# Attention queries for two tiles at once in a two-layer kernel, x transposed in pairs

## The reference, cut to what matters

```python
x = x + attention0(layernorm(x), ctx)          # q = xn @ Wq.T + bq, k, v from ctx, 16 heads of 16
x = x + ffn_sine(layernorm(x))                 # 256 -> 1024 -> 256
x = x + attention1(ctx, layernorm(x), mask)    # the same with a mask of 1024 x 77 for each batch
x = x + ffn_fp4(layernorm(x))                  # gate, up and down, 704 wide, values rounded to 4-bit floats
# attention: scores = q @ k.T / 4 per head, softmax over 77 keys, times v, then @ Wo + bo
```

## Time and profile before

| | before |
|---|---|
| median of 3 runs | 1034.82 us |
| runs | 1032.75 to 1035.31 us |
| profiled execution | 1034.89 us, span 1033.1 us |
| mean granted TensorE clock | 0.978 of full |
| TensorE matmuls busy | 961.5 us, 93% |
| VectorE busy | 834.7 us, 81% |
| ACT busy | 497.0 us, 48% |
| GpSimd busy | 467.5 us, 45% |

### The profile page before, as it was taken

How to read it: one execution, slowest core, us unless ns; L and a number is a source line. 1 busy time by engine, 2 the same in 40 slices (tenths; PEclk the granted TensorE clock), 3 DMA queues, 4 the chain that set the end, 5 groups by cost and what they waited for, 6 DMA issues and landing times. The chain is left out here.

```text
span 1033.1 us, 18658 instructions
## 1 busy us (share of the span) xinstructions
PE 961.5 (93%) x6532; PEld 869.5 (84%) x6532; DVE 834.7 (81%) x2049; ACT 497.0 (48%) x1061; POOL 467.5 (45%) x663
## 2 busy tenths in 40 slices
PE   6899999999589999998899999999957999999997
PEld 5899999999478888887699999999846888888885
DVE  4989999997499999986677777777666898898874
ACT  2554443433288888886344433333244544444442
POOL 1235445451366666653221211211026777777762
PEclk9999999999799999999999999999979999999999
DMA  9020000000000000001000000000000000000000
GB/s 348 10 93 2 2 2 1 1 2 2 0 1 1 2 1 1 1 1 44 7 1 2 1 2 1 2 1 1 2 1 0 21 2 22 21 22 21 22 21 21
DMA packets 6076, 18.21 MB, mean 18 GB/s; under 512 B 864, under 2 KB 2784, under 8 KB 5472
## 3 DMA queue, kind: packets, MB, share of 16 engines
q1 hardware_dynamic: 5264, 16.52, 4.2%
q10 hardware_dynamic: 720, 0.50, 0.2%
HBM read 12.83 MB, written 4.19 MB: 16 GB/s over the span
## 5 line engine op out<-in xcount | busy, mean ns | idle before, releaser
L662 ACT COPY a_xTs<-a_psQ 128x256 f32<-128x256 f32 x64 | 23.9, 373 | 266.4 <-PE a_psQ L734 266.4
L726 PE MATMUL a_psS<-kblk,a_qTs 128*128 128x308 f32 (+2 forms) x768 | 148.0, 338 | 1.4 <-DVE a_qTs L561 1.4
L795 PEld LDWEIGHTS a_psO<-vblk,a_prob 128*128 128x128 f32 x1280 | 148.4, 192 | 0.0
L795 PE MATMUL a_psO<-vblk,a_prob 128*128 128x51 f32 (+1 forms) x1280 | 148.2, 271 | 0.0
L1387 PE MATMUL f_psGU<-wgu,f_xTs 128*128 128x512 f32 (+1 forms) x576 | 141.3, 391 | 3.9 <-ACT f_silu L1339 2.7
L499 DVE TENSOR_REDUCE a_mx<-a_psS 128x6 f32<-128x462 f32 (+1 forms) x192 | 111.8, 583 | 19.6 <-PE a_psS L726 12.4
L726 PEld LDWEIGHTS a_psS<-kblk,a_qTs 128*128 128x128 f32 x768 | 119.2, 193 | 5.3 <-DVE a_qTs L561 1.6
L1387 PEld LDWEIGHTS f_psGU<-wgu,f_xTs 128*128 128x128 f32 x576 | 103.7, 192 | 19.9 <-DVE f_xTs L1151 4.6
L635 POOL TENSOR_TENSOR a_rstd<-a_mv,expo 128x1 f32<-128x1 f32 x64 | 16.4, 256 | 228.8 <-DVE a_mv L573 228.8
L1013 PEld LDWEIGHTS s_psY<-w,s_hid 128*128 128x128 f32 x768 | 97.4, 188 | 18.0 <-POOL s_hid L931 14.2
L1013 PE MATMUL s_psY<-w,s_hid 128*128 128x256 f32 x768 | 102.3, 282 | 6.7 <-POOL s_hid L931 6.7
(11 more groups left out here) (152 smaller groups left out, 1916.4 us busy)
## 6 DMA issues: line engine op xcount, KB each, us to landing
out_x<-x SPq DMA_DIRECT2D x8, 512.0 KB, 2.6
x<-in_x SPq DMA_DIRECT2D x3, 1024.0 KB, 12.5
w<-in_w SPq DMA_DIRECT2D x1, 2304.0 KB, 9.0
w<-in_w SPq DMA_DIRECT2D x2, 1024.0 KB, 17.3
a_mask<-in_mask SPq DMA_DIRECT2D x4, 308.0 KB, 4.0
wat<-in_att SPq DMA_DIRECT2D x1, 1024.0 KB, 20.3
x<-in_x SPq DMA_DIRECT2D x1, 768.0 KB, 8.5
wat<-in_att SPq DMA_DIRECT2D x2, 256.0 KB, 5.1
```

The costliest lines, as they stand in the source:

```text
L726: mm = nc.tensor.matmul(psS[n][:, (a - h0) * KV:(b - h0) * KV], qTs[:, u, p, k, :], kblk[:, r, t // R, k, (a - 8 * k) * KV:(b - 8 * k) * K ...
L795: mm = nc.tensor.matmul(psO[:, CH[c] * VW:(CH[c] + n) * VW], prob[:, v, c * P:(c + 1) * P], vblk[:, t // R, c * NJ * VW:(c * NJ + n) * VW] ...
```

## The change

Queries are made for a pair of tiles. In an even step i TensorE makes four x transposes, those of tiles i + 2 and i + 3, which fill the whole bank psQ; ACT copies all 512 columns to xTs, which is single now; and `queries(i + 2)` makes the first 128 query rows of both tiles at once, 256 columns wide, in the left half of psQ. In the odd step that follows there are no x transposes and no x copy, and `queries` makes the other 128 query rows, in the right half, after VectorE has read the left. ACT's bias (L683) and VectorE's low part (L561) are one instruction of 256 columns a step. qTs holds two pairs. Scores of a tile take their 128 of the 256 columns and wait for both halves.

All that comes before is moved: bn_stats, bn_aggr and the GpSimd pair to tile i + 5, normalise and the bias row to tile i + 4, and the steps begin at -5. VectorE runs steps -5 and -4 ahead of the key lows, step -3 ahead of the first keys, and steps -2 and -1 after the bias row (and the first mask). The waits for x loads are moved with bn_stats. vT is a view of the prob buffer, which is not written by exp before step 1.

The diff, cut (the headings after @@ say where):

```diff
@@ class Context: vT is handed in instead of allocated
-        self.vT = ctx.enter_context(nc.sbuf_tensor(f"b{l}_vT", [P, KC, B, 3 * KV], F32))
+        self.vT = vT
@@ attention, tiles
-        xTs = sb("xTs", [P, 2, KC * P])
-        qTs = sb("qTs", [P, 2, 2, KC, P], F32R)
+        xTs = sb("xTs", [P, KC, 2 * P])
+        qTs = sb("qTs", [P, 2, 2, KC, 2 * P], F32R)
...
-        FIRST, LAST, LOOP_FROM, LOOP_TO = ATT_FIRST, ATT_LAST, ATT_LOOP_FROM, ATT_LOOP_TO
+        FIRST, LAST, LOOP_FROM, LOOP_TO = ATT_FIRST - 2, ATT_LAST, ATT_LOOP_FROM, ATT_LOOP_TO
...
-        context = Context(nc, sem, g, l, ctx, psS[0:2], psT, (psO, psY))
+        vT = prob[:].rearrange("p u n -> p (u n)")[:, 0:KC * B * 3 * KV].rearrange("p (h b n) -> p h b n", h=KC, b=B)
+        context = Context(nc, sem, g, l, ctx, psS[0:2], psT, (psO, psY), vT)
@@ VectorE
-                def normalise(t, u):
+                def normalise(t):
+                    u = t % 2
                     wait(dve, rstd_ready, t + 1)
-                    wait(dve, xT_mm, t - 1)
+                    wait(dve, xT_mm, t // 2)
...
-                    if valid(i + 3):
-                        nc.vector.bn_stats(st[:, v, :], x[:, i + 3, :]).then_inc(st_set, 1)
-                        wait(dve, st_set, i + 4)
+                    if valid(i + 5):
+                        nc.vector.bn_stats(st[:, v, :], x[:, i + 5, :]).then_inc(st_set, 1)
+                        wait(dve, st_set, i + 6)
...
-                    if valid(i + 1):
-
-                        wait(dve, q_high, i + 2)
-                        for k in range(KC):
-                            last = nc.vector.scalar_tensor_tensor(
-                                qTs[:, v, 1, k, :], psQ[:, k * P:(k + 1) * P],
-                                cols[:, C_BQ + 2 * l + k:C_BQ + 2 * l + k + 1], qTs[:, v, 0, k, :].bitcast(F32),
-                                ALU.add, ALU.subtract)
-                        last.then_inc(q_low, 1)
+                    if valid(i + 2):
+                        s, h = (i + 2) // 2, i % 2
+                        wait(dve, q_high, i + 3)
+                        nc.vector.scalar_tensor_tensor(
+                            qTs[:, s % 2, 1, h, :], psQ[:, h * 2 * P:(h + 1) * 2 * P],
+                            cols[:, C_BQ + 2 * l + h:C_BQ + 2 * l + h + 1], qTs[:, s % 2, 0, h, :].bitcast(F32),
+                            ALU.add, ALU.subtract).then_inc(q_low, 1)
...
-                    if valid(i + 2):
-                        normalise(i + 2, u)
+                    if valid(i + 4):
+                        normalise(i + 4)
...
-                    if valid(i + 3):
+                    if valid(i + 5):
                         nc.vector.bn_aggr(mv[:, v, :], st[:, v, :]).then_inc(mv_ready, 1)
@@ VectorE, order before the loop
+                step(-5, 1)
+                step(-4, 0)
+                context.key_lows(dve)
                 step(-3, 1)
-                context.key_lows(dve)
-                step(-2, 0)
                 if inputs:
                     dve.wait_ge(inputs.in_const, 16 * 4)
                 context.first_keys_on_vector(dve)
                 context.bias_row(dve)
                 if l:
                     masks(0)
+                step(-2, 0)
                 step(-1, 1)
                 context.values(dve)
@@ GpSimd
-                    t = i + 3
+                    t = i + 5
@@ ACT
-                    if valid(i + 1):
-                        t = i + 1
-                        wait(act, xT_mm, t + 1)
-                        wait(act, q_mm, t - 1)
-                        nc.scalar.copy(xTs[:, v, :], psQ[:, 0:KC * P]).then_inc(xT_copied, 1)
+                    if valid(i + 2) and i % 2 == 0:
+                        s = (i + 2) // 2
+                        wait(act, xT_mm, s + 1)
+                        wait(act, q_mm, 2 * s)
+                        nc.scalar.copy(xTs[:].rearrange("p k n -> p (k n)"), psQ[:]).then_inc(xT_copied, 1)
...
-                        if n == 0 and valid(i + 1):
-                            t = i + 1
-                            wait(act, q_mm, t + 1)
-                            wait(act, score_mm, 3 * (t - 1))
-                            for k in range(KC):
-                                last = nc.scalar.activation(qTs[:, v, 0, k, :], psQ[:, k * P:(k + 1) * P], ACT.Identity,
-                                                            bias=cols[:, C_BQ + 2 * l + k:C_BQ + 2 * l + k + 1])
-                            last.then_inc(q_high, 1)
+                        if n == 0 and valid(i + 2):
+                            s, h = (i + 2) // 2, i % 2
+                            wait(act, q_mm, i + 3)
+                            wait(act, score_mm, 6 * (s - 1))
+                            nc.scalar.activation(qTs[:, s % 2, 0, h, :], psQ[:, h * 2 * P:(h + 1) * 2 * P], ACT.Identity,
+                                                 bias=cols[:, C_BQ + 2 * l + h:C_BQ + 2 * l + h + 1]).then_inc(q_high, 1)
@@ TensorE
-                    wait(pe, q_low, t + 1)
+                    s, part = t // 2, slice(t % 2 * P, (t % 2 + 1) * P)
+                    wait(pe, q_low, 2 * s + 2)
...
+                def x_transposes(s):
+                    wait(pe, xhat_ready, 2 * s + 2)
+                    wait(pe, q_low, 2 * s)
+                    for k in range(KC):
+                        for q in range(2):
+                            mm = nc.tensor.transpose(psQ[:, (2 * k + q) * P:(2 * k + q + 1) * P],
+                                                     xhat[:, q, k * P:(k + 1) * P], ident[:])
+                    mm.then_inc(xT_mm, 1)
+
+                def queries(n):
+                    s, h = n // 2, n % 2
+                    if valid(n):
+                        wait(pe, xT_copied, s + 1)
+                        if h == 1:
+                            wait(pe, q_low, n)
+                        for k in range(KC):
+                            mm = nc.tensor.matmul(psQ[:, h * 2 * P:(h + 1) * 2 * P], wat[:, k, h * P:(h + 1) * P],
+                                                  xTs[:, k, :], start=(k == 0), stop=(k == KC - 1))
                         mm.then_inc(q_mm, 1)
...
-                    if valid(i + 1):
-                        t = i + 1
-                        wait(pe, xhat_ready, t + 1)
-                        wait(pe, q_low, t)
-                        transpose_pair(psQ, xhat[:, v, :], xT_mm)
+                    if valid(i + 2) and i % 2 == 0:
+                        x_transposes((i + 2) // 2)
...
-                                queries(i + 1, v)
+                                queries(i + 2)
```

More of the change, by code:

```diff
@@ L127, with __init__ @@
 class Context:
-    def __init__(self, nc, sem, g, l, ctx, psK, psVT, psV):
+    def __init__(self, nc, sem, g, l, ctx, psK, psVT, psV, vT):
         self.nc, self.g, self.l, self.psK, self.psVT, self.psV = nc, g, l, psK, psVT, psV
@@ L545, in step @@
                         w4_scales(nc, dve, g, piece_of(i), u, 0)
-                    if l == 0 and i + 3 == 0:
+                    if l == 0 and i + 5 == 0:
                         dve.wait_ge(g["in_xa"], 16)
-                    if l == 0 and i + 3 == 2:
+                    if l == 0 and i + 5 == 2:
                         dve.wait_ge(g["in_x0"], 16)
-                    if l == 0 and i + 3 == R:
+                    if l == 0 and i + 5 == R:
                         dve.wait_ge(g["in_x"], 16 * (B - 1))
-                    if valid(i + 3):
-                        nc.vector.bn_stats(st[:, v, :], x[:, i + 3, :]).then_inc(st_set, 1)
-                        wait(dve, st_set, i + 4)
+                    if valid(i + 5):
+                        nc.vector.bn_stats(st[:, v, :], x[:, i + 5, :]).then_inc(st_set, 1)
+                        wait(dve, st_set, i + 6)
@@ L725, in scores @@
                                 for m, (p, r) in enumerate(((1, 0), (0, 1), (0, 0))):
-                                    mm = nc.tensor.matmul(psS[n][:, (a - h0) * KV:(b - h0) * KV], qTs[:, u, p, k, :],
+                                    mm = nc.tensor.matmul(psS[n][:, (a - h0) * KV:(b - h0) * KV], qTs[:, s % 2, p, k, part],
                                                           kblk[:, r, t // R, k, (a - 8 * k) * KV:(b - 8 * k) * KV],
@@ L735, in transpose_pair @@
                     mm.then_inc(done, 1)
-                def queries(t, u):
-                    if valid(t):
-                        wait(pe, xT_copied, t + 1)
-                        for h in range(KC):
-                            for k in range(KC):
-                                mm = nc.tensor.matmul(psQ[:, h * P:(h + 1) * P], wat[:, k, h * P:(h + 1) * P],
-                                                      xTs[:, u, k * P:(k + 1) * P],
-                                                      start=(k == 0), stop=(k == KC - 1))
+                def x_transposes(s):
[15 more added lines that the diff above has]
```

(1 more changed line is left out.)

## The result

The changed kernel took 1039.4 (median of 7 runs, 1037.0 to 1042.9), the kernel before 1035.0 (7 runs): ratio 1.005, 95% interval 1.0034 to 1.0067. It is slower by 0.5%. The forecast was +2.7, the measurement is +4.4. "Slower" by more than 0.3% had been given a chance of 0.48.

What follows compares the result with a forecast made beforehand. TensorE was taken to pace the loop, VectorE nearly tied. Steady steps +2.4, run-up +4.6, given back -1.4 and -1.5, end -1.4 sum to +2.7 on 1034.89: 1037.6 us, range 1032.5 to 1041.5 (the forecast's own 1034.5 to 1040).

Steps and rivals of the forecast that it cites:

- Steady steps, +2.4: Loop steps of both attention stages: a pair 0.09 longer, the longer x-copy wait outweighing savings from wider passes; +2.4 us.
- The pass price: Query passes on TensorE: 216 ns for 256 columns against 2 x 112, saving only 0.06 us per pair.
- The others, no price: VectorE, ACT and the shared prob buffer: none holds TensorE in the loop, ACT margin 0.5 us; no cost.
- Run-up adds +4.6: Start of both attention stages: both halves of the first pair come first, value copies start 2.3 us later in each; +4.6.
- rival 1: Run-up: idle TensorE brings a further low-clock stretch, costing 1 to 1.6 us per stage; 1040 to 1041, chance 0.20.
- Stage 1 gives back -1.5: First steps of stage 1: exp and step 2's scores 2.4 us earlier, gain at most 2.3, half of 1.6 lost to clock; -1.5.
- Attention 1 gives back -1.4: Steps 0 and 1 of the second attention stage: step 0 shorter by 1.2 us, step 1 by 0.22; -1.4.
- End -1.4: Step 30 of each attention stage no longer has queries: -0.65 us each, 0.05 more in the second; -1.4.
- Rival 2: First stage loop: VectorE, not TensorE, sets the pace, so 3.4 us is gained there; 1033.0, chance 0.10.
- Rivals 3 and 4: Loop queries: first, the x-copy wait vanishes, 1029.2, chance 0.05; second, wide passes near the fp32r price, 1018, chance 0.02.
- Rival 5: Even loop steps: ACT's backlog reaches TensorE, 0.25 us lost per pair; 1045, chance 0.05.

Runs made afterwards that it cites:

- early transposes: Changed kernel with TensorE's four x transposes moved ahead of the third bank of scores in even steps; 1033.1 us, ratio 0.9986 to the kernel before.
- narrow passes: Changed kernel with the pair's queries as 16 passes of 128 columns instead of 8 of 256; 1042.7 us, ratio 1.0076 to the kernel before.
- buffer control: Kernel before with only the transposed values placed in the prob buffer; ratio 1.0005 to the kernel before.
- coefficients edit: Changed kernel with VectorE making the rotary coefficients behind step 4 instead of step 0 of the first stage; ratio 1.0034 to the kernel before.
- again: The changed kernel unchanged, run on another chip; 1039.1 us, ratio 1.005 to the kernel before.
- two orders moved: Changed kernel with ACT's value copies ahead of the second query half's bias and x transposes ahead of the third score bank; 1024.4 us, ratio 0.9899.
- three-edit kernel: Changed kernel with value copies before the second half's bias, x transposes before the third score bank, rotary coefficients behind step 4; 1023.0 and 1024.3 us.

## Why the prediction was right, and where it was not

The time fell in the range, above the forecast's 1037.6, near the top of the forecast's own range of 1034.5 to 1040. The direction and the largest terms were right; that the sum came so near is in part luck, since errors of opposite sign met in it.

- **Steady steps, +2.4: right.** +2.41. Even 7.67 and odd 6.95 where 7.66 and 6.93 were said, the copy 585 ns for 0.588, ACT's and VectorE's 256-column reads 474 and 481 ns for 0.47 and 0.48. The experiment with early transposes removed 0.28 and 0.29 a pair where the wait was put at 0.29. Groups by line and form of the changed kernel:

```profile
L562 DVE SCALAR_TENSOR_TENSOR a_qTs<-a_psQ,cols,a_qTs 128x256 fp32r<-128x256 f32 x64 | 30.8, 481 | 7.0 <-ACT a_qTs L684 5.9
L684 ACT ACTIVATE a_qTs<-a_psQ,cols 128x256 fp32r<-128x256 f32 x64 | 30.3, 474 | 28.2 <-PE a_psQ L754 28.2
L664 ACT COPY a_xTs<-a_psQ 128x512 f32<-128x512 f32 x32 | 18.7, 585 | 147.3 <-PE a_psQ L743 147.3
```

- **The pass price: right.** The narrow passes cost 0.058 a pair. The estimate of 98 ns from the Trainium skill, "TensorE: Matmul & The Clock Gate", section "Back-to-back issue gap", does not hold for these f32 passes: four take 1.03 in the row of the early transposes, that is three of 0.217 and a last one of 0.38 with its drain.
- **The others, no price: right.** No gap behind ACT or VectorE in the loop, and the buffer control is at 1.0005. One reading was loose: "VectorE needs some 7.13" is the step less 0.12, not VectorE's busy time, which was 6.79 a step and is now 7.08 and 6.36, so it had more room than that. TensorE came to its first x transposes at 13.38, against 13.61 in the earlier trace rows.
- **Run-up adds +4.6: too small.** +2.53 and +4.25 in the profiled execution, +3.15 and +2.42 in the other. The chain itself is 2.59, 0.28 over the forecast: 0.1 at the end of each query group (ACT's bias starts 1.17 and 1.13 after the group's first pass, where 1.07 and some 1.05 were taken) and 0.1 from VectorE's low part to the next pass (500.66 to 500.81, where 0.05 was taken). What came on top in stage 1 is rival 1: the second half's passes and the first value transposes ran at the lower clock behind the idle stretches. I had argued that the value transposes lose less than half by it; 53 passes took 2.9 more. Rival 1 was right in mechanism, in part of its size.
- **Stage 1 gives back -1.5: the step that failed.** +0.15 and -0.32. "Now it starts at once, so exp and the scores of step 2 come some 2.4 earlier" is right for the exp: it starts 7.94 after the first scores, against 10.28 before (37.32 - 29.38 and 35.41 - 25.13), 2.34 earlier. It is wrong for the scores, which came 0.52 earlier (12.84 against 13.36), because it took the exp for the last thing that they need. They also need the low part of their queries, which VectorE makes in step 1 in both kernels, behind the weights' low parts and the rotary coefficients. It was over 12.78 after the first scores before, and 12.78 after them in the changed kernel: nothing had made VectorE's queue shorter, and its 0.58 to spare became a wait of 1.65. The prediction gave this low part no price; it looked for VectorE's limit in `on`, a step later. So it is not the pairing that holds tile 2, but the next wait in line once the exp was early. The coefficients edit shows it: 1.45 back in step 1. Step 2 then took 0.92 more (0.45 in "again") with its scores at half clock, for which half of 1.6 stood in the forecast, and step 3 gave 0.25.
- **Attention 1 gives back -1.4: mechanism right, size off.** -2.3. Step 0 gave 1.23 for 1.2. Step 1 gave 1.09 instead of 0.22. Of this 0.54 is TensorE's wait for the exp with the transposes around it (513.03 to 514.22 before, 519.50 to 520.15 now), since the table load, which stood right ahead of the late exp in the earlier trace rows, now runs before its input is there; 0.22 are the x transposes, and the rest is the wait for the x copy and the shorter query group. The prediction had counted the x transposes alone. ACT's row and the transposes it awaits, in the changed kernel:

```profile
517.40 1.28 ACT L678 ACT_TABLE_LOAD   x1
...
518.83 0.60 ACT L678 ACTIVATE a_prob<-a_psT 128x512 f32<-128x512 f32 x1 [0.15 <-PE a_psT L777]
```

```profile
518.20 0.60 PE L777 MATMUL a_psT<-ident,a_shifted 128*128 128x128 f32 x4
```

  In the kernel before it stood in ACT's queue behind the x copy of the same step, which waited for TensorE's x transposes; an odd step now has no x copy, so the load starts behind the key blocks and TensorE's wait for the exp (0.32 in the earlier trace rows) is gone.
- **End -1.4: right.** -0.63 and -0.71.
- **Rival 2** (VectorE paces stage 1): no; shorter TensorE groups shortened the step at once. **Rivals 3 and 4**: no by the copy's 585 ns and the pass price; hiding the wait by order instead is worth 8.7 over the same 29 pairs, which rival 3 priced at 8.4. **Rival 5**: no gap.

In short: the forecast's errors were -0.9 (attention 1's steps), +1.7 (stage 1's steps) and, in the profiled run, +2.2 (run-ups); their sum with +1.0 from the other stages is 4.0, which is that run's +6.7 less the forecast's +2.7.

## What to carry to other kernels

Making an operand for two tiles at once halves the number of hand-overs but lengthens each, so it pays only if the wider copy has a wider cover: move its producer up ahead of independent work, and let other copies go ahead of the second half in the run-up. Here the change alone lost 0.5% and with two orders moved it gained 1.0%. The unpaired kernel gains 0.4% by its own early x transposes, and against that one the pairing is worth only 0.04 us a pair in the loop. When a change removes the wait that ends last, read what else the same instruction needs and how much that had to spare, also in the first steps, where one-time work sits: here 0.58 was left, and 2.4 was claimed. And compare the pieces of the trace as well as the medians, each piece from the start of its stage: a stretch of low clock that has left one piece may stand in the one before it.

## What the runs showed of the hardware

The place of low clock is not fixed by the kernel alone: in two executions of the three-edit kernel the stretch from the first query pass to the first scores ran at 0.85 and 1.00, and steps 0 to 3 at 1.00 and 0.94. Its amount goes with most of the scatter. Of 29 runs of the kernel before on one chip, those with a mean granted clock of 0.980 took 1032.0 to 1034.9 and those at 0.973 to 0.974 took 1036.2 to 1038.7; at 0.975 they lie between, 1033.9 to 1038.2. So the time of a single execution says little about an edit worth 1.

A switch of ScalarE's table costs 1.28 here. In the kernel before, the load starts 0.02 after the copy ahead of it (511.61 + 0.37 to 512.00) and the exp 0.01 after the load (513.29). In the changed kernel the exp follows 0.15 after it, since TensorE's transposes come that late. The Trainium skill, "ScalarE: Activation LUTs", section "What ACT_TABLE_LOAD costs", has 1.28 for the load, which agrees, and 1.38 for a drain besides; no row here shows that drain.
